# First attention of an audio tower: where the weighted-value products, the projections and the way back stand in a slot

## The reference

```python
h = h + _L0_attn_ref(_layernorm(h, axis=-1), L0_attn_Q, L0_attn_K, L0_attn_VO)

def _L0_attn_ref(x, Q, K, VO):           # x: 16 x 255 x 64, 8 heads, R = 32
    q = jnp.einsum('btd,hrd->bhtr', x, Q)
    k = jnp.einsum('bud,hrd->bhur', x, K)
    scores = jnp.einsum('bhtr,bhur->bhtu', q, k) / sqrt(d)
    attn = jax.nn.softmax(scores, axis=-1)
    ctx = jnp.einsum('bhtu,bud->bhtd', attn, x)
    out = jnp.einsum('bhtd,hde->bte', ctx, VO)
    return out
```

## Time and profile before

| | us |
|---|---|
| median of 3 runs | 820.14 (819.86 to 825.51) |
| the profiled execution | 823.06 |
| its span, first to last instruction | 821.1 |
| TensorE busy (matmuls) | 660.8, 80% |
| VectorE busy | 616.1, 75% |
| ScalarE busy | 497.5, 61% |
| GpSimd busy | 334.4, 41% |
| first attention, first scores to last product | about 94 to 326 |

### The profile page before, as it was taken

The page is one execution under the profiler, slowest core; times in us unless marked ns, Lnnn a source line. Parts: engine busy times, 40 slices in busy tenths (PEclk is TensorE's granted clock), DMA queues, the critical chain, the costliest instruction groups (busy, mean ns, idle before and its releaser), DMA issues. The chain is left out here.

```text
span 821.1 us, 16347 instructions
## 1 busy us (share of the span) xinstructions
PE 660.8 (80%) x4968; PEld 371.8 (45%) x4968; DVE 616.1 (75%) x1685; ACT 497.5 (61%) x1246; POOL 334.4 (41%) x410
## 2 busy tenths in 40 slices
PE   0503599999999998999988886475888888889996
PEld 0403266666666665223333222462555555557332
DVE  6678178888888988488889997653788888867653
ACT  2455377776767673466666774533877777763552
POOL 1003156777777786522233332443244444430000
PEclk9999999999999999799999998687999999995999
DMA  4003000000000000343232321000000000000001
GB/s 99 0 9 95 0 1 2 1 0 0 0 0 0 0 0 2 116 170 98 95 93 94 100 93 55 2 0 1 2 1 0 0 0 0 0 2 1 8 20 25
DMA packets 21749, 24.36 MB, mean 30 GB/s; under 512 B 12358, under 2 KB 12614, under 8 KB 21446
## 3 DMA queue, kind: packets, MB, share of 16 engines
q1 hardware_dynamic: 19463, 23.31, 9.3%
q10 hardware_dynamic: 2239, 0.49, 0.3%
HBM read 22.48 MB, written 1.31 MB: 29 GB/s over the span
## 5 line engine op out<-in xcount | busy, mean ns | idle before, releaser
L1309 POOL TENSOR_TENSOR big<-big 128x1024 f32<-128x1024 f32 x64 | 120.5, 1894 | 68.2 <-DVE big L1188 68.2
L1006 ACT ACTIVATE big<-ps,big 128x255 f32<-128x255 f32 x256 | 117.8, 487 | 9.4 <-DVE big L1182 9.3
L975 ACT ACTIVATE big<-ps,b1s 128x512 f32<-128x512 f32 x128 | 80.6, 681 | 39.8 <-PE ps L759 39.7
L1182 DVE TENSOR_REDUCE big<-ps 128x4 f32<-128x1020 f32 x64 | 74.6, 1206 | 32.6 <-PE ps L822 32.6
L1859 DVE TENSOR_REDUCE big<-ps 128x4 f32<-128x1020 f32 x64 | 78.0, 1218 | 11.4 <-PE ps L1500 6.6
L1195 DVE COPY mid<-ps 128x512 f32<-128x512 f32 x128 | 81.9, 680 | 5.5 <-DVE res L1200 2.9
L998 ACT ACTIVATE big<-ps 128x512 f32<-128x512 f32 x64 | 39.5, 618 | 68.2 <-PE ps L810 41.5
L759 PE MATMUL ps<-big,wall 64*128 64x512 f32 x256 | 77.8, 673 | 0.7 <-ACT big L946 0.7
L769 PE MATMUL ps<-big,w2s 128*64 128x512 f32 x256 | 71.5, 638 | 8.0 <-ACT big L975 8.0
L1766 ACT ACTIVATE big<-ps 128x1024 f32<-128x1024 f32 x64 | 65.8, 1029 | 13.6 <-PE ps L1506 9.0
L832 PE MATMUL ps<-cst,big 128*128 128x128 f32 x512 | 71.3, 279 | 2.7 <-DVE mid L1195 1.6
(11 more groups left out here) (265 smaller groups left out, 1365.0 us busy)
## 6 DMA issues: line engine op xcount, KB each, us to landing
mid<-spread_w SPq DMA_DIRECT2D x128, 128.0 KB, 2.8
mid<-in_split_sel SPq DMA_DIRECT2D x1, 1536.0 KB, 7.2
wall<-in_w SPq DMA_DIRECT2D x1, 1280.0 KB, 7.8
out_tokens<-res SPq DMA_DIRECT2D x16, 56.0 KB, 1.6
cst<-in_consts SPq DMA_DIRECT2D x1, 648.5 KB, 7.0
mid<-in_w_raw SPq DMA_DIRECT2D x1, 620.0 KB, 5.6
w2s<-in_w SPq DMA_DIRECT2D x1, 512.0 KB, 3.2
mid<-in_taps ACTq DMA_DIRECT2D x1, 320.0 KB, 3.8
```

The costliest lines, as they stand in the source:

```text
L975: last = nc.scalar.activation(hid[e % 2][j], H1(e, j), ACT.Relu, bias=b1s[0][:, 2 * e + j:2 * e + j + 1])
L1006: last = nc.scalar.activation(e_sb[r % 4][:, jj, tq, 0:NW], S[:, 2 * (r % 2) + jj, tq, 0:NW], ACT.Exp, scale=-1.0, bias=minus[r % 4][:, jj ...
L1182: nc.vector.tensor_reduce(minus[r % 4], S[:, 2 * a:2 * a + 2, :, 0:NW], AX.X, ALU.min).then_inc(s_mx, 1)
L1309: nc.gpsimd.tensor_tensor(e_sb[r % 4], e_sb[r % 4], bc(inverse[r % 4].unsqueeze(3), [P, 2, 2, 256]), ALU.mult).then_inc(s_A, 1)
```

## The change

Each slot's work stays the same; its order changes.

- TensorE: the order is now scores, first projection, turn 2k, second projection, turn 2k + 1, at g = 1 the way back, then the products of rounds 2k - 1 and 2k one behind the other. The wait of the way back on `s_out` now counts the second projection's copy, and the wait for the addition (`s_add`), which guards the shared bank, moves from the second projection at g = 1 to the first at g = 0.
- ScalarE: the copy of the second projection moves from the start of the next slot into its own: at g = 1 between the two rounds' exponentials, at g = 0 to the slot's end, behind `o_out`, which itself moves behind the second round's exponentials.
- VectorE: at g = 1 the addition moves behind the second round's copy, ahead of the second inverse, and the norm's preparation behind that inverse.

GpSimd and SyncE are unchanged.

```diff
--- before.py
+++ after.py
@@ -863,23 +863,23 @@
                         if more or par == 0:
                             if g == 0:
                                 pe.wait_ge(s_xs, b + 2)
+                                if not known or b >= 2:
+                                    pe.wait_ge(s_add, b - 1)
                             project(*first_of(k), FIRST + 2 * N)
                         turn(2 * k, 2 * N)
-                        if g == 1 and (not known or b >= 1):
-                            pe.wait_ge(s_O, b)
-                            pe.wait_ge(s_out, 2 * N + (2 if not more and par == 1 else 6))
-                            outputs_turn(1 - par)
-                        if not known or N >= 1:
-                            outputs(2 * k - 1, 2 * N - 1)
                         if route:
                             route()
                         if more or (par, g) == (0, 0):
                             if g == 1:
                                 pe.wait_ge(s_xs, b + 3)
-                                if not known or b >= 1:
-                                    pe.wait_ge(s_add, b)
                             project(*second_of(k), FIRST + 2 * N + 1)
                         turn(2 * k + 1, 2 * N + 1)
+                        if g == 1 and (not known or b >= 1):
+                            pe.wait_ge(s_O, b)
+                            pe.wait_ge(s_out, 2 * N + (7 if more else 6 if par == 0 else 2))
+                            outputs_turn(1 - par)
+                        if not known or N >= 1:
+                            outputs(2 * k - 1, 2 * N - 1)
                         if g == 0:
                             if not known or N >= 1:
                                 pe.wait_ge(s_out, 2 * N + 4)
@@ -1019,12 +1019,14 @@
                         par, g = at(k)
                         b = 2 * j + par
 
-                        if (not known or N >= 1) and (more or (par, g) in ((0, 0), (0, 1))):
-                            if g == 1 and (not known or b >= 1):
-                                act.wait_ge(s_PV, 2 * QUADS * b)
-                            if g == 0 and (not known or b >= 1):
-                                act.wait_ge(s_S, 2 * b)
-                            project_out(*second_of(k - 1), FIRST + 2 * N - 1)
+                        def second_out():
+                            if more or (par, g) == (0, 0):
+                                if g == 0 and (not known or b >= 1):
+                                    act.wait_ge(s_PV, 2 * QUADS * b)
+                                if g == 1:
+                                    act.wait_ge(s_S, 2 * b + 2)
+                                project_out(*second_of(k), FIRST + 2 * N + 1)
+
                         if more or par == 0:
                             if g == 0 and (not known or b >= 1):
                                 act.wait_ge(s_S, 2 * b)
@@ -1033,10 +1035,14 @@
                             project_out(*first_of(k), FIRST + 2 * N)
                         if more or k < 2 * QUADS - 1:
                             exps(2 * k + 2, 2 * N + 2)
+                        if g == 1:
+                            second_out()
+                        if more or k < 2 * QUADS - 1:
+                            exps(2 * k + 3, 2 * N + 3)
                         if g == 0 and (not known or b >= 1):
                             o_out(b - 1, 1 - par)
-                        if more or k < 2 * QUADS - 1:
-                            exps(2 * k + 3, 2 * N + 3)
+                        if g == 0:
+                            second_out()
                         if then:
                             then()
 
@@ -1209,22 +1215,22 @@
                             dve.wait_ge(s_S, N + 2)
                             maxima(2 * k + 2)
                             maxima(2 * k + 3)
+                        copy(2 * k, 2 * N)
+                        if unit:
+                            inverses(2 * k + 2, 2 * N + 2)
+                        if route:
+                            route()
+                        copy(2 * k + 1, 2 * N + 1)
                         if g == 1 and (not known or b >= 1):
                             add(b - 1)
                             dve.wait_ge(s_add, b)
-                        copy(2 * k, 2 * N)
                         if unit:
-                            inverses(2 * k + 2, 2 * N + 2)
+                            inverses(2 * k + 3, 2 * N + 3)
                         if g == 1 and (not known or b >= 1):
                             norm.stats(res[:, span(2 * (b - 1), 2)])
                             if not known or b >= 2:
                                 dve.wait_ge(s_nx, b - 1)
                             norm.variance()
-                        if route:
-                            route()
-                        copy(2 * k + 1, 2 * N + 1)
-                        if unit:
-                            inverses(2 * k + 3, 2 * N + 3)
 
                     for n in range(4):
                         nc.vector.memset(e_sb[n][:, :, :, NW:NW + 1], 0.0).then_inc(s_pad, 1)
```

## The result

The changed kernel takes 850.34 us (median of 4 runs, 846.73 to 851.89), the kernel before 820.0 on the same occasion: ratio 1.0348, 95% interval [1.0293, 1.0403]. The forecast was 848.4 within 836 to 857. The profiled execution took 850.99, its span 849.0 (821.1 before).

What follows compares the result with a forecast made beforehand. TensorE was taken to set the pace, with VectorE's chain close behind. Slots of 8.05 and 7.84 made 15.89 us a batch, + 27.3 over 14 batches, + 28.3 in all: 848.4 us, range 836 to 857.

Steps and rivals of the forecast that it cites:

- slot g = 1: First slot of a steady batch, scores to scores: 7.36 us plus 0.48 for the way back, 7.84.
- slot g = 0: Second slot of a steady batch, scores to scores: 8.05 us, with the second product held until 7.03.
- last batch and what follows: Last batch's first slot longer by about 1.3, the slot after it offsetting; 0 for both, between -1 and +1.3.
- The turn without cover: Second turn, behind one projection only, waits some 0.9 us for VectorE's copies; first product then stands at 5.39.
- The output copy: At g = 0 the second product waits for ScalarE to copy the first's bank: 7.03 in place of 6.34.
- Two products in a row: On TensorE, the first of two neighbouring products costs 0.95 us, the second 1.02; merging itself saves 0.16 a slot.
- Way back, projection copies, addition: Way back adds 0.48 at g = 1, its wait covered by 0.2; ScalarE's projection copies and VectorE's addition cost 0.
- TensorE as the bound: Rival: TensorE stays the bound and 0.16 is saved in some 29 slots, 815.5 us; chance 0.08.
- Half of the loss: Rival: wait for the output copy hidden or far smaller, batch 15.20, + 18.6, 838.7 us; chance 0.12.
- The hold by GpSimd: Rival: GpSimd's weighing holds VectorE's L591, level today; 0.5 longer gives 855.5 us; chance 0.15 including similar waits.
- The prediction's section on the bound: Before the change TensorE has 13.2 of 14.0 us filled, waiting 0.53 for VectorE and 0.22 for ScalarE.
- that rival: Rival: TensorE's clock falls in part because of its waits, giving 860 us and more; chance 0.03.

Runs made afterwards that it cites:

- Experiment 1: Changed kernel, but in slots g = 0 the products stand apart again and ScalarE's output copy sits between the exponentials; 828.55 us, ratio 1.0124.
- experiment 9: Changed kernel, but VectorE copies the first turn between the two minima instead of behind them, in every slot; 863.12 us, ratio 1.0514.
- Experiment 5: Changed kernel with products apart in both slots, output copy between the exponentials, and the norm's addition of 1e-5 (L591) left out; 817.67 us, ratio 0.9952.
- experiment 8: Kernel before the change, with the addition of 1e-5 to the variance (L591) left out of the first attention's norm; 815.36 us, ratio 0.9928.
- experiment 4: Changed kernel with products apart in both slots and output copy between the exponentials, other moves kept; 831.25 us, ratio 1.0142.
- experiment 7: Changed kernel with products apart in slots g = 0 only, output copy between the exponentials, and L591 left out; 826.68 us, ratio 1.0074.
- experiment 6: Changed kernel with the addition of 1e-5 to the variance (L591) left out of the first attention's norm; 848.8 us, ratio 1.0316.
- experiment 3: Changed kernel, but with the products apart again in slots g = 1 only, slots g = 0 staying merged; 857.34 us, ratio 1.0483.
- experiment 2: Changed kernel with products apart in slots g = 0, but ScalarE's output copy left behind both groups of exponentials; 842.97 us, ratio 1.0282.

## Why the prediction was right, and where its terms were off

Per batch and in all, forecast beside what the profile after shows:

| term | forecast | measured |
|---|---|---|
| second turn behind the scores | 4.16, the end of the first copy | 4.21, 4.22 |
| first product behind the scores, g = 0 | 5.39 | 5.41 |
| slot g = 1 | 7.84 | 7.67 |
| slot g = 0 | 8.05 | 8.16 and 8.26 |
| batch, mean of 14 | 15.89 | 15.86 |
| slot g = 1 of batch 0, more than before | 0.95 | 0.87 |
| last batch and what follows | 0 (-1 to +1.3) | +0.1: +1.0, then -0.9 |
| sum in the profiled execution | +28.3 | +27.9 |

The 15.86 beside 15.89 is in part luck. The slot g = 1 was forecast 0.17 too long and the slot g = 0 some 0.16 too short, and the two errors cancel. The medians differ by 30.3 where the profiled executions differ by 27.9; the runs of one kernel lie as much as 6 us apart, so the terms explain the profiled pair and no finer.

*The turn without cover.* Right to 0.02 us at the first product. Experiment 1 takes this wait from the slots g = 0 and experiment 9 from all. Only the first gains, because it takes the wait for the output copy away too, while experiment 9 makes that one longer.

*The output copy.* The mechanism was right and the term 0.2 too small. Batch 1, whose slots are written out, has the forecast's slot to 0.02: scores at 116.46 and 124.49, 8.03. In the loop it is 8.16 or 8.26. There the copy starts 0.13 behind the product and not 0.04, and the second product 0.13 or 0.23 behind the copy and not 0.12. One difference is that in the loop the values waited for are computed from the loop's counter. Whether this is the cause of the 0.1 and 0.2, and why the batches of even number take the 8.26, was not tried and stays open.

*Two products in a row.* Mis-sized the other way: from 225.56 to 227.44 the pair is 1.88, so if the second costs the 1.02 that it costs ahead of another shape, the first costs 0.86, under the lower bound of 0.93 that I had worked out from its own busy time. The way back's block was 0.49 (225.07 to 225.56), not 0.57. Together these are the 0.17 of the slot g = 1. The Trainium skill names a drain on a change of tiling mode (TensorEngine Tiling (Array Packing), Key Properties). The rows agree with it: a product costs 0.16 more when it leaves its shape, 1.02 against 0.86, and the turn ahead of it 0.09 more, 0.96 against 0.87; that this is a drain is not seen by itself. A merged pair so saves 0.25 a slot of TensorE's work, not the 0.16 of the prediction. It is shorter than each of the two waits that came with it (0.78 and 0.75 in the rows above).

*Way back, projection copies, addition.* The forecast's 0 for the copies and the addition holds nearly. No wait stands at the way back (225.07 above). Experiment 5 has the moves of the way back, the projection copies and the addition, without the hold and without merged products: 13.75 a batch, 0.11 more than experiment 8, which is without the moves. Which of them the 0.11 belongs to was not tried.

*The rivals.* TensorE as the bound is refuted by every slot above. Half of the loss would have needed the output copy hidden; among the orders built on the changed kernel it is hidden only where the products stand apart and the copy stands between the exponentials (experiments 1, 4, 5 and 7). The hold by GpSimd was forecast as level with the scores' path, and is: nothing in experiments 6 and 7, 13.6 us in experiment 4. L591 ends with the weighing inside which it starts: 213.35 beside 213.32 before the change, 228.76 beside 228.74 after it, 232.74 beside 232.71 in experiment 3. The Trainium skill's lock on the shared port pair (SBUF — State Buffer, Who interferes with whom) fits these three pairs. So VectorE and GpSimd meet here at more than semaphores. The hold also cost the kernel before the change 5 us or a little more, 0.37 a batch. The prediction's section on the bound did not say so, though its rows show it: VectorE's minima start late behind L591, TensorE's wait of 0.53 follows from that, and it goes in experiment 8. The wait of 0.22 stays there and is not its consequence.

*The tail.* The last batch's slot g = 0 took 9.35 (338.43 to 347.78). Before the change it took 6.79, so it is 2.56 longer, where about 1.3 was forecast:

```profile
342.73 1.17 PE L832 MATMUL ps<-cst,big 128*128 128x128 f32 x8 [2.13 <-DVE mid L1201]
...
345.87 1.98 PE L849 MATMUL ps<-mid,big 128*64 128x256 f32 x8 [0.52 <-issue]
...
347.78 1.09 PE L910 MATMUL ps<-cst,big 128*128 128x128 f32 x8
```

TensorE's clock fell there (granted clock 0.66 from 345 to 349), and the second product took 1.91 to the next block in place of 1.02. The last slot was 1.55 shorter than before, so the batch is 1.0 longer, and what follows the attention was 0.9 shorter. The forecast's 0 for all of it was met, but not by the way that it gave: the clock was no part of it.

## What to carry to other kernels

Before two blocks are moved together, list for each buffer what has to happen between its writer and its next writer on other engines, and count that round trip as a block of its own: here 0.4 us of copy, with the hops to it and back, made the first product's step 0.87 or 0.97 longer, where the merge saved 0.25. A wait of TensorE has to be priced with what stands next behind it, as experiment 9 gained nothing from removing one at the cost of a later copy; and a small VectorE operation that runs long and ends with GpSimd's is a thing to place between GpSimd's instructions, which gave 0.64% for one moved line.

## What the hardware showed that I had not expected

In two orders with longer waits inside a slot, TensorE's clock fell from 2.4 to 1.2 GHz in the middle of the stage. In experiment 3, where a slot g = 0 has waits of 1.63 and 0.64, the clock fell once in the loop. The waits of that slot, and the profiled execution in stretches of 2 us:

```profile
216.74 1.25 PE L832 MATMUL ps<-cst,big 128*128 128x128 f32 x8 [1.63 <-DVE mid L1203]
...
220.10 1.97 PE L849 MATMUL ps<-mid,big 128*64 128x256 f32 x8 [0.64 <-ACT big L1016]
```

The columns below are the stretch, its length, the busy time (and instructions) of TensorE, its weight load, VectorE, ScalarE and GpSimd, the granted clock, the DMA share and GB/s:

```profile
216.00:218.00 2.00, 1.26 (x10) 0.92 (x12) 1.84 (x5) 2.00 (x11) 1.32 (x3) 1.00 0.00 0
218.00:220.00 2.00, 1.46 (x8) 0.49 (x8) 0.98 (x3) 1.23 (x6) 2.00 (x2) 0.60 0.00 0
220.00:222.00 2.00, 1.90 (x8) 0.77 (x9) 0.00 (x0) 0.46 (x1) 1.74 (x2) 0.50 0.00 0
222.00:224.00 2.00, 2.00 (x18) 1.22 (x16) 0.00 (x0) 0.00 (x0) 0.00 (x0) 0.50 0.00 0
224.00:226.00 2.00, 2.00 (x14) 1.25 (x11) 1.84 (x2) 0.54 (x2) 0.00 (x0) 0.69 0.00 0
226.00:228.00 2.00, 2.00 (x18) 1.24 (x17) 1.71 (x4) 1.88 (x9) 0.00 (x0) 1.00 0.00 0
```

The slot in question took 10.32 and the next 8.58, for 8.98 and 7.06: 2.9 us for one fall. The other eleven slots g = 0 of the loop have waits of the same size and keep 1.00, and experiment 2, with a wait of 1.24 in each slot g = 0, keeps it from 110 to 310 us as well. So the waits alone do not decide it, and what does is not shown. In experiment 9 the clock fell several times (0.89 from 140 to 155 and from 170 to 200). Its 14 batches took 231.75 in the profiled execution, where 16.09 a batch would be 225.3: 6.5 us. The last batch and what follows took 5 us more than in the changed kernel; why was not looked into.

The changed kernel itself, with waits of 0.8 in each slot, keeps 1.00 from 110 to 310 us in the profiled execution; from 110 us on its only fall within the first attention is in the last batch, behind a wait of 2.13. The forecast had given that rival 3 in 100 for the changed kernel. It did not occur in the steady part, but experiments 3 and 9 show that a kernel with somewhat longer waits in a slot can meet it.
